# Decoder layer, FFN part: turning the quantised rows of blocks 1 to 7 by transposing DMAs from SBUF to SBUF

## Chip, cores and metric

The kernel runs on one core of one Trainium2 chip, in one launch. The metric is the device time in microseconds (us). Most repeated executions of one kernel lie within 0.3% of each other.

## What is computed

The reference is one post-norm decoder layer over x of 4 x 1024 rows of 512 numbers: attention, a retention-like cross attention, and an FFN whose activations and weights are quantised to 8-bit integers. Each is followed by a residual sum and a layernorm. The change is in the FFN only:

```python
def _act_fake_quant(x, clip_factor):
    scale = sigmoid(clip_factor) * max(abs(x)) / 127.0
    return clip(round(x / scale), -128.0, 127.0) * scale

xq = _act_fake_quant(x, clip_x[0])                       # x: 4096 rows of 512
gate = einsum('bsh,ih->bsi', xq, _weight_fake_quant(w_gate))   # I = 1408
up = einsum('bsh,ih->bsi', xq, _weight_fake_quant(w_up))
h = _act_fake_quant(silu(gate) * up, clip_down[0])
y = einsum('bsi,hi->bsh', h, _weight_fake_quant(w_down))
x = _layernorm(x + y)
```

The scale of h needs the largest |h| over all rows, so every gate and up product comes before the first down product.

## The kernel before

Three phases run one after the other: `attention_phase`, `retention_phase`, `ffn_phase`. The FFN runs from about 1551 us to the end at 1814.5 us of the profiled span. It has a gate/up stage (to about 1716 us) and a down stage.

**Gate/up stage.** The 4096 rows are 8 blocks (`NB`) of 512 rows. A block is four tiles of 128 rows x 512 numbers, each a source `("x", blk, k)`. For each tile:

- SP loads the rows from `x2d` (line 2798) into `lead` or `rows`, in turn by block;
- ACT scales and rounds them to int8 (`f_i`, "round", line 2845);
- DVE or ACT casts them to bf16 integers (`f_xq`, "cast.d" line 2905, "cast.a" line 2850), four buffers;
- TensorE turns the tile by four 128x128 transposes into a PSUM bank (`f_tr`, "turn", line 3015), two banks;
- DVE (block 0, line 2910) or ACT (blocks 1 to 7, line 2855) copies the bank into the block's `f_xqT` ("copy.d", "copy.a"). `f_xqT` has two buffers of 128 x 4 x 512, for even and odd blocks.

With all four tiles of a block in `f_xqT`, TensorE makes 11 pairs (`IT`) of a gate and an up product, each four matmuls with 128x512 operands into one of six PSUM banks (`f_pj`, line 3026). ACT makes the silu of the gate bank (`f_sg`, line 2862), DVE multiplies it by the up bank into `f_h` (line 2923), and DVE takes the largest magnitude of that tile (`f_hm`, line 2928). Five blocks of h stay in SBUF. Blocks 0, 1 and 2 are spilled to `h_scratch` by one DMA of 2816 KB each (line 2809) when their last tile has its maximum.

**Down stage.** After block 7 the maximum over all of h gives the second scale ("top"). Then h is rounded, cast and multiplied by the down weights (lines 3045, 3055), and residual, layernorm statistics and the output follow.

**What sets the order.** `ffn_plan` simulates the FFN with a planned length for each piece of work and writes one list for each engine's queue (SP, ACT, DVE, POOL, PE). Engines then take their list strictly in order. The tile preparation of block b (`turned`) is placed among the gate/up pairs of block b-1, at b-0.6 to b-0.36 for the four turns. The function `lighter()` gives a cast or a copy to ACT when ACT has less planned work waiting than DVE. SP's list holds all DMAs of the phase. `Passed` leaves out a wait that the engine has already passed.

The lines that matter for the turn before (TensorE, and the wait of the first product of a block):

```python
            elif kind == "turn":
                src = key[0]
                w.wait_ge(*made_whole(src))
                if tr.before[src]:
                    w.wait_ge(*copied(tr.before[src]))
                for f in range(4):
                    m = pe.transpose(tbank[tr.at[src]][:, f * P:(f + 1) * P], xqb[xq.at[src]][:, f * P:(f + 1) * P],
                                     identb[:, :])
                m.then_inc(turn_mm, 1)
            elif kind in ("gate", "up"):
                blk, i = key
                for k in range(4):
                    w.wait_ge(*copied(("x", blk, k)))
```

Of the kernel before, what the change touches and what calls it, by code (L numbers as in the profile page):

```python
# [18 lines left out]
IT = I // P  # L19
# [2388 lines left out]
def ffn_plan():  # L2408

    flow = Flow()  # L2410
    flow.rank, flow.alone = FRANK, ("cast.d",)
    put, after = flow.put, flow.after
    pj, tr, xq, i8 = Slots(6), Slots(2), Slots(4), Slots(3)
    done, copier, caster = set(), {}, {}
    T, G, N = [], [], []
    loads = []

    def has(*keys):
        return all(k in done for k in keys)
# [9 lines left out]
    def turned(src, place, ready):  # L2429

        def made():
            xq.give(src)
            copier[src] = "copy.a" if src[1] and lighter() else "copy.d"
            put("ACT" if copier[src] == "copy.a" else "DVE", (copier[src], src), 0.5 if copier[src] == "copy.a" else 0.36, copied,
                lambda: has("sdrmm") if src[1] == 1 else src[1] < 2 or has(("upmm", src[1] - 2, IT - 1)))

        def copied():
            tr.give(src)
            done.add(("copy", src))
        N.append((place - 0.12, lambda: integers(src, 512, ready, lambda: done.add(("whole", src)))))  # L2440
        pe_item(T, place, ("turn", src), 0.24, made, lambda: room(tr) and has(("whole", src)), lambda: tr.take(src))

    def lighter():

        load = {e: max(flow.free[e] - flow.now, 0) + sum(p[1] for p in flow.ready[e]) for e in ("ACT", "DVE")}
        return load["ACT"] + 0.3 < load["DVE"]
# [201 lines left out]
    for e in flow.order:  # L2648
        for it, n in numbered(flow.order[e]).items():
            assert num.setdefault(it, n) == n or it[0] == "top", it  # L2650
    return flow.order, flow.yields, num, copier, caster, pj, tr, xq, i8


def ffn_phase(nc, A, x2d, hd, amax, wsc, wq, keep, out):
    ph = Phase(nc, "f")
    sb = ph.sb
    order, yields, num, copier, caster, pj, tr, xq, i8 = ffn_plan()

    identb, identf, ones, sig = keep.identb, keep.identf, keep.ones, keep.sig
    eps = sb("eps", [P, 1], F32)  # L2660
# [21 lines left out]
    xr_in, out_done = [ph.sem(f"xr_in{i}") for i in range(16)], [ph.sem(f"out{i}") for i in range(16)]  # L2682
    gu_in = [ph.sem(f"gu{i}_in") for i in range(IT)]
    d_in = [ph.sem(f"d{i}_in") for i in range(4)]
    spilled, back_in = ph.sems("spill0 spill1 spill2"), ph.sems("back0 back1 back2")
    turn_mm, gate_mm, up_mm, top_mm, sdr_mm, d_mm = ph.sems("turn_mm gate_mm up_mm top_mm sdr_mm d_mm")
    round_act, cast_act, copy_act, silu_act, sd_act, tn_act = ph.sems(
        "round_act cast_act copy_act silu_act sd_act tn_act")
    top_dve, cast_dve, copy_dve, gsc_pool, h_dve = ph.sems(
        "top_dve cast_dve copy_dve gsc_pool h_dve")  # L2690
    diag_pool, sdr_dve, r_dve, bn_dve, ag_dve, rs_dve = ph.sems("diag_pool sdr_dve r_dve bn_dve ag_dve rs_dve")
# [46 lines left out]
    def place_free(w, src):  # L2738

        if src[0] == "h":  # L2740
            if src[1] >= 2:
                w.wait_ge(d_mm, num[("down", src[1] - 2, 3)])
        elif xq.before[src]:
            w.wait_ge(turn_mm, num[("turn", xq.before[src])])

    def target(src):

        return xqT[src[1] % 2][:, :, src[2] * P:(src[2] + 1) * P]

    def copied(src):  # L2750

        kind = copier[src]
        return (copy_act if kind == "copy.a" else copy_dve), num[(kind, src)]

    def after(key):

# [25 lines left out]
    def sync(sp):  # L2782
        w = Passed(sp)
        for it in order["SP"]:
            kind, key = it[0], it[1:]
            if kind == "rows":
                m, k = key
                i, r0 = place_of(m, k), block_of(m) * 512 + k * P
                if m == 1:
                    for j in range(4):  # L2790
                        w.wait_ge(keep.x2_out[j], 16 * len(HALVES))
                if 2 <= m < NB + 2:
                    w.wait_ge(round_act, num[("round", ("x", m - 2, k))])
                elif m >= NB + 4:
                    w.wait_ge(out_done[i], 16)
                elif m >= NB + 2:
                    w.wait_ge(up_mm, NGATED)
                sp.dma_start(xr[i][:, :], x2d[r0:r0 + P, :]).then_inc(xr_in[i], 16)
            elif kind == "gu":
                i = key[0]  # L2800
                sp.dma_start(wgu[:, i, :, :], wq["gu"][i]).then_inc(gu_in[i], 16)
            elif kind == "d":
                c = key[0]
                sp.dma_start(wd[:, c, :, :], wq["d"][c]).then_inc(d_in[c], 16)
            elif kind == "spill":
                blk = key[0]
                w.wait_ge(h_dve, num[("gated", blk, IT - 1)])
                w.wait_ge(peak_dve, num[("peak", blk, IT - 1)])
                sp.dma_start(hd[blk], hs[place(blk)][:, :, :]).then_inc(spilled[blk], 16)
            elif kind == "back":  # L2810
                m = key[0]
                for lo, _ in ffn_pieces():
                    w.wait_ge(round_act, num[("round", ("h", m, lo))])
                w.wait_ge(spilled[SPILL[m]], 16)
                sp.dma_start(hs[m][:, :, :], hd[SPILL[m]]).then_inc(back_in[m], 16)
            elif kind == "tn":
                m, k = key
                i, r0 = place_of(NB + m, k), SECOND[m] * 512 + k * P
                w.wait_ge(tn_act, num[it])
                sp.dma_start(out[r0:r0 + P, :], xr[i][:, :]).then_inc(out_done[i], 16)  # L2820
        for i in range(16):
            w.wait_ge(out_done[i], 16 * (NB // 4))

    def scalar(act):
        w = Passed(act)
        for it in order["ACT"]:
            kind, key, n = it[0], it[1:], num[it]
            if kind == "init":
                act.activation(scr[:, 0:2], sig[:, :], ACT.Silu)
            elif kind == "round":  # L2830
                src = key[0]
                if i8.before[src]:
                    w.wait_ge(*made_whole(i8.before[src]))
                if src[0] == "x":
                    m, k = src[1:]
                    w.wait_ge(*arrived(m, k))
                    w.wait_ge(top_dve, 4)
                    r = scr[:, 8:9]
                else:
                    m = src[1]  # L2840
                    w.wait_ge(top_dve, 8)
                    if m >= KEEP:
                        w.wait_ge(back_in[m - KEEP], 16)
                    r = scr[:, 9:10]
                act.activation(byte(src), source(src), ACT.Copy, scale=r).then_inc(round_act, 1)  # L2845
            elif kind == "cast.a":
                src = key[0]
                w.wait_ge(round_act, num[("round", src)])
                place_free(w, src)
                act.activation(integer(src), byte(src), ACT.Copy).then_inc(cast_act, 1)  # L2850
            elif kind == "copy.a":
                src = key[0]
                w.wait_ge(turn_mm, num[("turn", src)])
                copy_free(w, src)
                act.activation(target(src), turned_bank(src), ACT.Copy).then_inc(copy_act, 1)
            elif kind == "gated":
                blk, i = key
                w.wait_ge(gate_mm, n)
                w.wait_ge(gsc_pool, 2)
                if n > 3:  # L2860
                    w.wait_ge(h_dve, n - 3)
                act.activation(sg[(n - 1) % 3][:, :], bank[pj.at[("gate", *key)]][:, :], ACT.Silu, scale=gsc[:, i:i + 1]
                               ).then_inc(silu_act, 1)
            elif kind == "norm":
                m, k0 = key
                end = normed_rows(m, k0)[1]
                c, e = 4 * (m % 2) + k0, 4 * (m % 2) + end
                w.wait_ge(init_pool, 1)
                for k in range(k0, end):
                    w.wait_ge(ag_dve, num[("stats", m, k)])  # L2870
                if m >= 2:
                    w.wait_ge(rs_dve, 2 * num[("norm", m - 2, 0)])
                act.activation(sd[:, c:e], ag[m % 2][:, k0:end, 1], ACT.Sqrt, bias=eps[:, 0:1]).then_inc(sd_act, 1)  # L2873
            elif kind == "tn":
                m, k = key
                c, i = 4 * (m % 2) + k, place_of(NB + m, k)
                w.wait_ge(rs_dve, 2 * num[("norm", m, normed_rows(m, k)[0])])
                act.activation(xr[i][:, :], xr[i][:, :], ACT.Identity, bias=mr[:, c:c + 1], scale=rs[:, c:c + 1]  # L2878
                               ).then_inc(tn_act, 1)

    def vector(dve):
        w = Passed(dve)
        for it in order["DVE"]:
# [22 lines left out]
            elif kind == "copy.d":  # L2906
                src = key[0]
                w.wait_ge(turn_mm, num[("turn", src)])
                copy_free(w, src)
                dve.tensor_copy(target(src), turned_bank(src)).then_inc(copy_dve, 1)  # L2910
            elif kind == "gated":
                blk, i = key
# [249 lines left out]
```

## Time and profile before

| | us |
|---|---|
| median of 3 runs | 1816.25 (1816.05 to 1820.79) |
| the profiled execution's own time | 1816.41 |
| its span | 1814.5 |
| TensorE busy in the span | 1673.4 (92%) |
| DVE busy | 1342.6 (74%) |
| ACT busy | 1064.6 (59%) |
| POOL busy | 1067.0 (59%) |
| mean granted TensorE clock | 0.982 of full |

The span runs from the first to the last instruction. The profiled execution took 1.91 us more than its span, and its time lies 0.16 us above the median. Busy shares are averages over three phases with different limits, so the rows below are taken from the FFN alone. Times in them count from the start of the span.

### The profile page before, as it was taken

Reading aid. Unit: us, or ns where it says so; the run is one execution under the profiler, and the core shown is the slowest. Engines: PE = TensorE matmul, PEld = TensorE weight load, DVE = VectorE, ACT = ScalarE, POOL = GpSimd, SP = SyncE. Lnnn points to the kernel's source line nnn. Section 1 sums busy time; section 2 is a strip of 40 time slices with the busy share of each in tenths; the row PEclk is TensorE's granted clock in tenths of the full one; section 3 lists DMA queues with packets and bytes.
Section 4 is the critical chain, followed back from the end, with each engine's and each line's share of the span. In section 5 each row is a group of like instructions: output and inputs, shape, how many; then the busy total and the mean of one; then the engine's idle time right before and its main releaser. Section 6 shows DMA issues by size and latency. Waiting matters only on the chain. (4 is left out here: it accounts for less than half of the span.)

```text
span 1814.5 us, 37213 instructions
## 1 busy us (share of the span) xinstructions
PE 1673.4 (92%) x13410; PEld 761.8 (42%) x13426; DVE 1342.6 (74%) x3006; ACT 1064.6 (59%) x1889; POOL 1067.0 (59%) x1020
## 2 busy tenths in 40 slices
PE   5999999989999999998796999999999998799997
PEld 2433343334433344333233555555555554344443
DVE  6777657786677856677784777778678667788898
ACT  6476555665556655566642557565465454565587
POOL 4088777588685867869862765665675656000044
PEclk9999999999999999999998999999999999899999
DMA  8312102231013310222325223232232131651275
GB/s 289 117 27 82 31 22 57 77 105 30 23 49 90 98 31 24 81 66 59 93 94 167 65 86 103 92 105 96 88 110 77 59 112 48 229 219 49 68 264 207
DMA packets 123039, 172.02 MB, mean 95 GB/s; under 512 B 22376, under 2 KB 73064, under 8 KB 121960
## 3 DMA queue, kind: packets, MB, share of 16 engines
q1 hardware_dynamic: 117192, 160.91, 27.6%
q10 hardware_dynamic: 5664, 8.73, 1.6%
q8 instruction: 107, 1.75, 0.4%
q14 instruction: 76, 0.62, 0.1%
HBM read 106.12 MB, written 38.14 MB: 80 GB/s over the span
## 5 line engine op out<-in xcount | busy, mean ns | idle before, releaser
L1165 DVE CUSTOM_DVE_ANT_0 a_mx<-a_mx,a_mqk 128x128 f32<-128x128 f32 (+3 forms) x512 | 242.2, 512 | 137.0 <-PE a_mx L1365 133.3
L980 ACT ACTIVATE a_P<-a_mx 128x512 f32<-128x512 f32 (+3 forms) x417 | 186.9, 495 | 134.4 <-PE a_mx L1383 75.2
L1379 PE MATMUL a_mx<-a_Qs,a_Ks 128*128 128x512 f16 (+3 forms) x768 | 228.7, 333 | 18.3 <-ACT a_P L980 7.5
L1248 POOL TENSOR_TENSOR a_P<-a_P 128x512 f32<-128x512 f32 (+3 forms) x189 | 183.8, 1000 | 101.4 <-PE a_o L1395 76.7
L1365 PE MATMUL a_mx<-a_Ks,a_Qs 96*128 96x512 f16 (+3 forms) x768 | 223.5, 330 | 5.9 <-DVE a_nm L1165 2.4
L1248 POOL TENSOR_TENSOR a_P<-a_P,share 128x512 f32<-128x512 f32 (+3 forms) x199 | 185.5, 961 | 24.5 <-ACT share L980 18.1
L980 ACT ACTIVATE share<-a_mx 128x512 f32<-128x512 f32 (+3 forms) x303 | 135.9, 495 | 99.5 <-PE a_mx L1383 58.1
L1168 DVE TENSOR_REDUCE a_nm<-a_mx 128x1 f32<-128x512 f32 x256 | 165.0, 683 | 31.9 <-PE a_mx L1365 31.0
L2277 PE MATMUL r_pj<-share,cth 128*128 128x512 f16 x672 | 167.1, 382 | 2.8 <-PEq L123 2.3
L2277 PE MATMUL r_pj<-r_xTh,share 128*128 128x512 f16 x512 | 159.1, 382 | 3.2 <-DVE r_xTl L2123 3.0
L3026 PE MATMUL f_pj<-f_xqT,f_wgu 128*128 128x512 bf16 x688 | 154.5, 379 | 1.6 <-DVE f_xqT L2910 0.8
L1248 POOL TENSOR_TENSOR share<-share,a_P 128x512 f32<-128x512 f32 (+3 forms) x152 | 137.0, 932 | 20.1 <-ACT a_P L980 12.4
L1379 PEld LDWEIGHTS a_mx<-a_Qs,a_Ks 128*128 128x128 f16 x768 | 71.7, 98 | 170.1 <-issue 72.9
L2993 POOL TENSOR_TENSOR lead<-lead,f_sg 128x512 f32<-128x512 f32 x8 | 10.1, 1270 | 183.5 <-DVE f_sg L2943 177.9
L1365 PEld LDWEIGHTS a_mx<-a_Ks,a_Qs 96*128 96x128 f16 x768 | 71.0, 98 | 91.9 <-issue 14.3
L1259 POOL TENSOR_TENSOR a_Ol<-a_on,a_Oh 128x512 f16<-128x512 f32 x32 | 37.9, 1184 | 119.9 <-ACT a_Oh L997 116.3
L1383 PE MATMUL a_mx<-a_mkq,identb 128*128 128x128 bf16 x512 | 107.1, 221 | 0.0
L3026 PEld LDWEIGHTS f_pj<-f_xqT,f_wgu 128*128 128x128 bf16 x704 | 67.6, 98 | 76.9 <-DVE f_xqT L2910 0.7
L1276 PE MATMUL a_mx<-share,a_wkh 128*128 128x512 f16 x256 | 83.8, 391 | 15.9 <-DVE share L1027 15.3
L1276 PE MATMUL a_mx<-share 128*128 128x512 f16 x384 | 97.1, 379 | 1.0 <-DVE a_on L1199 0.9
L2277 PE MATMUL r_pj<-r_xTl,share 128*128 128x512 f16 x256 | 97.6, 381 | 0.0
L2277 PEld LDWEIGHTS r_pj<-share,cth 128*128 128x128 f16 x672 | 62.8, 98 | 75.1 <-issue 5.8
(309 smaller groups left out, 4019.7 us busy)
## 6 DMA issues: line engine op xcount, KB each, us to landing
x_scratch<-rows SPq DMA_DIRECT2D x60, 256.0 KB, 2.1
rows<-x_scratch SPq DMA_DIRECT2D x56, 256.0 KB, 4.3
lead<-in_xT SPq DMA_DIRECT2D x24, 512.0 KB, 4.6
lead<-in_ctxT SPq DMA_DIRECT2D x38, 256.0 KB, 2.8
h_scratch<-f_h SPq DMA_DIRECT2D x3, 2816.0 KB, 9.1
f_h<-h_scratch SPq DMA_DIRECT2D x3, 2816.0 KB, 10.2
a_Ks<-a_kph SPq DMA_DIRECT2D x256, 32.0 KB, 1.9
a_Qs<-a_qph SPq DMA_DIRECT2D x256, 32.0 KB, 1.9
```

The lines of the kernel that those rows point to most:

```text
L980: act.activation(Pf[pf.at[key]][:, off:512], pb[:, off:512], ACT.Exp).then_inc(p_exp, 1)
L1165: dve.tensor_tensor_reduce(bank_of(it)[:, 0:n], bank_of(it)[:, 0:n], mqk[:, 512 - n:512], 1.0, -3e38, ALU.add, ALU.max, nm[:, col:col + 1] ...
L1168: dve.tensor_reduce(nm[:, col:col + 1], bank_of(it)[:, 0:n], AXX, ALU.max).then_inc(max_dve, 1)
L1248: pool.tensor_tensor(total[:, off:512], total[:, off:512], Pf[pf.at[key]][:, off:512], ALU.add).then_inc(add_pool, 1)
L1259: pool.tensor_tensor(Ol[:, g, cs], onb[on.at[key]][:, :], Oh[:, g, cs], ALU.subtract).then_inc(o_lo, 1)
L1276: m = pe.matmul(out, u, v, start=(n == 0), stop=(n == 11))
L1365: pe.matmul(pb[:, 0:n], Qs[s][0:96, j, qt * P:(qt + 1) * P], Ks[s][0:96, j, hf * 512:hf * 512 + n], start=True, stop=True).then_inc(max_mm, 1)
L1379: m = pe.matmul(pb[:, off:512], Ks[s][:, j, kt * P:(kt + 1) * P], Qs[s][:, j, qb * 512 + off:(qb + 1) * 512], start=True, stop=not diag)
L1383: m = pe.matmul(pb[:, off:off + P], identb[:, :], mkq[:, :], start=False, stop=True)
L2277: m = pe.matmul(out, u, v, start=(i == 0), stop=(i == 11))
L2993: pool.tensor_tensor(xr[i][:, :], xr[i][:, :], sg[(NGATED + n - 1) % 3][:, :], ALU.add).then_inc(y_pool, 1)
L3026: m = pe.matmul(bank[pj.at[it]][:, :], wgu[:, i, k0 + k, :], xqT[blk % 2][:, k, :], start=(k == 0), stop=(k == 3))
```

## The change

For the tiles of blocks 1 to 7 the planner no longer plans a "turn" on TensorE and a copy by ACT. When the bf16 tile `f_xq` is whole, it gives SP an item "turnd": a DMA that transposes the 128x512 tile into its place in `f_xqT`, SBUF to SBUF. The planner reckons 1.25 us of SP and 1.8 us more until it has landed. TensorE's products wait for the DMA's semaphore instead of for the copy's. The wait that protects `f_xqT` (`copy_free`) moves from ACT to SP, and the wait for a free `f_xq` buffer is now for the DMA that read it. Block 0 is turned as before.

```diff
         def made():
             xq.give(src)
-            copier[src] = "copy.a" if src[1] and lighter() else "copy.d"
-            put("ACT" if copier[src] == "copy.a" else "DVE", (copier[src], src), 0.5 if copier[src] == "copy.a" else 0.36, copied,
-                lambda: has("sdrmm") if src[1] == 1 else src[1] < 2 or has(("upmm", src[1] - 2, IT - 1)))
+            put("DVE", ("copy.d", src), 0.36, copied)
...
-        N.append((place - 0.12, lambda: integers(src, 512, ready, lambda: done.add(("whole", src)))))
+
+        def landed():
+            xq.give(src)
+            done.add(("copy", src))
+
+        def whole():
+            done.add(("whole", src))
+            if src[1]:
+                put("SP", ("turnd", src), 1.25, lambda: after(1.8, landed),
+                    lambda: has("sdrmm") if src[1] == 1 else has(("upmm", src[1] - 2, IT - 1)))
+        N.append((place - 0.12, lambda: integers(src, 512, ready, whole)))
+        if src[1]:
+            return
         pe_item(T, place, ("turn", src), 0.24, made, lambda: room(tr) and has(("whole", src)), lambda: tr.take(src))
...
+    turn_in = [ph.sem(f"turn{i}_in") for i in range(8)]
...
         elif xq.before[src]:
-            w.wait_ge(turn_mm, num[("turn", xq.before[src])])
+            w.wait_ge(*turned(xq.before[src]))
...
+    def turned(src):
+
+        if src[1]:
+            return turn_in[4 * (src[1] % 2) + src[2]], 16 * ((src[1] + 1) // 2)
+        return turn_mm, num[("turn", src)]
+
     def copied(src):
 
-        kind = copier[src]
-        return (copy_act if kind == "copy.a" else copy_dve), num[(kind, src)]
+        return turned(src) if src[1] else (copy_dve, num[("copy.d", src)])
...
+            elif kind == "turnd":
+                src = key[0]
+                w.wait_ge(*made_whole(src))
+                copy_free(w, src)
+                sp.dma_start_transpose(target(src), xqb[xq.at[src]][:, :]).then_inc(turn_in[4 * (src[1] % 2) + src[2]], 16)
```

**SP's list, start of the FFN.** In these rows `f_wgu` and `f_wd` are the weights of gate/up and of down, `lead` and `rows` the x tiles of even and odd blocks, `f_h` a block of h on its way to `h_scratch`. Before:

```order
771 L2798 DMA rows<-x_scratch 128x512 x4
772 L2804 DMA f_wd<-d_scratch 128x1408 x4
773 L2798 DMA lead<-x_scratch 128x512 x4
774 L2809 DMA h_scratch<-f_h 128x5632
775 L2798 DMA rows<-x_scratch 128x512 x4
```

Now:

```order
771 L2814 DMA rows<-x_scratch 128x512 x4
772 L2820 DMA f_wd<-d_scratch 128x1408
773 L2825 DMA_TRANSPOSE f_xqT<-f_xq 128x4x128
774 L2820 DMA f_wd<-d_scratch 128x1408
775 L2825 DMA_TRANSPOSE f_xqT<-f_xq 128x4x128
776 L2820 DMA f_wd<-d_scratch 128x1408
777 L2825 DMA_TRANSPOSE f_xqT<-f_xq 128x4x128
778 L2820 DMA f_wd<-d_scratch 128x1408
779 L2825 DMA_TRANSPOSE f_xqT<-f_xq 128x4x128
780 L2814 DMA lead<-x_scratch 128x512 x4
781 L2830 DMA h_scratch<-f_h 128x5632
782 L2825 DMA_TRANSPOSE f_xqT<-f_xq 128x4x128 x4
783 L2814 DMA rows<-x_scratch 128x512 x4
```

The four turns of block 1 stand between the loads of the down weights, the x tiles of block 2 come behind them, and the four turns of block 2 stand directly behind the spill of block 0, ahead of the x tiles of block 3. The groups of block 3 and 4 stand in the same way behind the spills of blocks 1 and 2.

**ACT's list, one block.** `f_i` is the int8 tile. Before:

```order
1191 L2845 ACTIVATE f_i<-lead,f_scr 128x512 x2
1192 L2862 ACTIVATE f_sg<-f_pj,f_gsc 128x512
1193 L2855 ACTIVATE f_xqT<-f_tr 128x4x128
1194 L2845 ACTIVATE f_i<-lead,f_scr 128x512
1195 L2862 ACTIVATE f_sg<-f_pj,f_gsc 128x512
1196 L2855 ACTIVATE f_xqT<-f_tr 128x4x128
1197 L2845 ACTIVATE f_i<-lead,f_scr 128x512
1198 L2862 ACTIVATE f_sg<-f_pj,f_gsc 128x512
1199 L2855 ACTIVATE f_xqT<-f_tr 128x4x128
1200 L2862 ACTIVATE f_sg<-f_pj,f_gsc 128x512
1201 L2855 ACTIVATE f_xqT<-f_tr 128x4x128
```

Now:

```order
1187 L2866 ACTIVATE f_i<-lead,f_scr 128x512 x2
1188 L2878 ACTIVATE f_sg<-f_pj,f_gsc 128x512
1189 L2866 ACTIVATE f_i<-lead,f_scr 128x512
1190 L2878 ACTIVATE f_sg<-f_pj,f_gsc 128x512
1191 L2866 ACTIVATE f_i<-lead,f_scr 128x512
1192 L2878 ACTIVATE f_sg<-f_pj,f_gsc 128x512
1193 L2871 ACTIVATE f_xq<-f_i 128x512
1194 L2878 ACTIVATE f_sg<-f_pj,f_gsc 128x512 x8
```

The four copies are gone, and the cast of the fourth tile, DVE's before, is now ACT's. On DVE this is one cast less in each of blocks 1 to 7. On TensorE the 28 turns between the products are gone, and the 704 matmuls of the gate/up stage stand in one row:

```order
+L3048 MATMUL f_pj<-f_xqT,ones 128x128 x4
+L3030 MATMUL f_tr<-identb,f_xq 128x128 x16
+L3041 MATMUL f_pj<-f_xqT,f_wgu 128x512 x704
+L3020 MATMUL f_pj<-identf,f_scr 1x128
```

From the first instruction of the down stage on, the lists of ACT, DVE, PE and POOL are the same as before. SP's differs there in nothing either.

## Rows read from the trace of the kernel before

**Rows 1.** The page, the span in 40 equal slices: TensorE and its clock.

```profile
PE   5999999989999999998796999999999998799997
PEclk9999999999999999999998999999999999899999
```

**Rows 2.** Busy time of each engine, blocks 1, 4 and 7 of gate/up.

```profile
core 0: us, PE busy (x) PEld busy (x) DVE busy (x) ACT busy (x) POOL busy (x), PEclk, DMA share, GB/s
...
1577.80:1597.70 19.90, 19.79 (x103) 9.52 (x104) 16.88 (x26) 11.86 (x20) 0.00 (x0) 1.00 0.52 199
...
1637.50:1657.40 19.90, 19.79 (x104) 9.50 (x105) 16.87 (x26) 11.87 (x20) 0.00 (x0) 1.00 0.20 54
...
1697.20:1716.30 19.10, 19.05 (x88) 8.46 (x87) 15.79 (x22) 7.57 (x11) 0.00 (x0) 1.00 0.01 2
```

**Rows 3.** The chain of waits, block 1 and the start of block 2.

```profile
1577.63 8.15 PE f_pj L3026 x37
1585.78 0.22 PE f_tr L3015 x4
1586.00 1.73 PE f_pj L3026 x8
1587.73 0.22 PE f_tr L3015 x4
...
1591.63 0.22 PE f_tr L3015 x4
...
1597.52 2.54 PE f_pj L3026 x11
```

**Rows 4.** Groups of instructions by shape, 1557 to 1717 us.

```profile
L2923 DVE SCALAR_TENSOR_TENSOR f_h<-f_pj,f_usc,f_sg 128x512 f32<-128x512 f32 x88 | 66.0, 750 | 17.9 <-PE f_pj L3026 12.5 <-ACT f_sg L2862 4.4
L2862 ACT ACTIVATE f_sg<-f_pj,f_gsc 128x512 f32<-128x512 f32 x88 | 60.2, 684 | 53.5 <-PE f_pj L3026 53.5
L2928 DVE TENSOR_REDUCE f_hm<-f_h 128x1 f32<-128x512 f32 x87 | 59.6, 686 | 2.7
L2855 ACT ACTIVATE f_xqT<-f_tr 128x512 bf16<-128x512 bf16 x28 | 16.7, 598 | 14.8 <-PE f_tr L3015 14.8
L2905 DVE CAST f_xq<-f_i 128x512 bf16<-128x512 int8 x28 | 11.8, 420 | 4.8 <-ACT f_i L2845 4.8
```

**Rows 5.** Instructions in order of time: casts of block 1, spill, casts of block 2.

```profile
1564.92 0.43 DVE L2905 CAST f_xq<-f_i 128x512 bf16<-128x512 int8 x1 [0.83 <-ACT f_i L2845]
...
1579.61 0.32 SPq L2809 DMA_DIRECT2D h_scratch<-f_h  x1
1579.97 5.56 SPq L2798 DMA_DIRECT2D rows<-x_scratch  x4
...
1583.89 0.42 DVE L2905 CAST f_xq<-f_i 128x512 bf16<-128x512 int8 x1
...
1589.31 0.42 DVE L2905 CAST f_xq<-f_i 128x512 bf16<-128x512 int8 x1
```

**Rows 6.** DMA issues: KB each, median us from issue to landing.

```profile
h_scratch<-f_h SPq DMA_DIRECT2D x3, 2816.0 KB, 9.1
f_wd<-d_scratch SPq DMA_DIRECT2D x4, 352.0 KB, 8.5
a_Ks<-a_kph SPq DMA_DIRECT2D x256, 32.0 KB, 1.9
```

**Rows 7.** The page, DMA queues: packets, MB, share of 16 engines' span.

```profile
q1 hardware_dynamic: 117192, 160.91, 27.6%
```

**Rows 8.** The x loads of the FFN, from the view of line 2798.

```profile
DMA to landing us min/median/max: 2.6/4.1/10.8
```

**Rows 9.** Instructions in order of time, from the gate/up stage into the down stage.

```profile
1716.36 0.75 DVE L2923 SCALAR_TENSOR_TENSOR f_h<-f_pj,f_usc,f_sg 128x512 f32<-128x512 f32 x1 [0.25 <-PE f_pj L3026]
1717.15 0.69 DVE L2928 TENSOR_REDUCE f_hm<-f_h 128x1 f32<-128x512 f32 x1
...
1719.76 11.74 ACT L2845 ACTIVATE f_i<-f_h,f_scr 128x512 int8<-128x512 f32 x12 [3.58 <-DVE f_scr L2900]
```

**Rows 10.** Busy time of each engine in the down stage.

```profile
1717.00:1757.00 40.00, 33.70 (x140) 14.29 (x141) 33.37 (x61) 31.09 (x34) 12.72 (x10) 0.91 0.82 305
1757.00:1797.00 40.00, 39.26 (x182) 17.25 (x179) 39.31 (x81) 34.84 (x43) 20.28 (x16) 1.00 0.54 188
```

More of the change, by code:

```diff
@@ L2413, in ffn_plan @@
     pj, tr, xq, i8 = Slots(6), Slots(2), Slots(4), Slots(3)
-    done, copier, caster = set(), {}, {}
+    done, caster = set(), {}
     T, G, N = [], [], []
@@ L2650, in ffn_plan @@
             assert num.setdefault(it, n) == n or it[0] == "top", it
-    return flow.order, flow.yields, num, copier, caster, pj, tr, xq, i8
+    return flow.order, flow.yields, num, caster, pj, tr, xq, i8
 def ffn_phase(nc, A, x2d, hd, amax, wsc, wq, keep, out):
@@ L2656, in ffn_phase @@
     sb = ph.sb
-    order, yields, num, copier, caster, pj, tr, xq, i8 = ffn_plan()
+    order, yields, num, caster, pj, tr, xq, i8 = ffn_plan()
     identb, identf, ones, sig = keep.identb, keep.identf, keep.ones, keep.sig
@@ L2684, in ffn_phase @@
     d_in = [ph.sem(f"d{i}_in") for i in range(4)]
+    turn_in = [ph.sem(f"turn{i}_in") for i in range(8)]
     spilled, back_in = ph.sems("spill0 spill1 spill2"), ph.sems("back0 back1 back2")
     turn_mm, gate_mm, up_mm, top_mm, sdr_mm, d_mm = ph.sems("turn_mm gate_mm up_mm top_mm sdr_mm d_mm")
-    round_act, cast_act, copy_act, silu_act, sd_act, tn_act = ph.sems(
-        "round_act cast_act copy_act silu_act sd_act tn_act")
+    round_act, cast_act, silu_act, sd_act, tn_act = ph.sems(
+        "round_act cast_act silu_act sd_act tn_act")
     top_dve, cast_dve, copy_dve, gsc_pool, h_dve = ph.sems(
@@ L2850, in scalar @@
                 act.activation(integer(src), byte(src), ACT.Copy).then_inc(cast_act, 1)
[L2851 to L2855, printed above, removed]
             elif kind == "gated":
@@ L2908, in vector @@
                 w.wait_ge(turn_mm, num[("turn", src)])
-                copy_free(w, src)
                 dve.tensor_copy(target(src), turned_bank(src)).then_inc(copy_dve, 1)
```

## The prediction

> **What bounds the kernel now.** I read the page's slices first. TensorE is busy at 9 tenths in most of them, and its clock shows 8 only in two [rows 1]. Averages over three phases don't tell what one stage is worth, so I went to the table by stretch. In block 1 TensorE is busy 19.79 of 19.90 us at clock 1.00, DVE 16.88, ACT 11.86 [rows 2]. The other blocks that hold turns look the same. Block 7, whose stretch holds 88 matmuls and no turns, takes 19.10 us. The chain of waits then tells whether the turns lie on the path or beside it: it runs along TensorE alone through a block, products, turn, products, and each turn (four transposes) stands in it with 0.22 us [rows 3]. There is no wait for a copy or for x tiles in it. So gate/up is bound by TensorE issuing its list without a gap, and whatever leaves that list shortens the stage, as long as nothing new stops the list.
>
> **What the change removes.** Four turns in each of seven blocks, 28 x 0.22 = **6.2 us** of TensorE's chain. A cross-check: a block with turns takes 19.89 us from product to product (1577.63 to 1597.52) [rows 3], so without its 4 x 0.22 it takes 19.0, and the stretch of block 7 has 19.10 with its drain [rows 2]. ACT loses 28 copies of 598 ns (16.7 us) and the 14.8 us that it sat waiting for turns [rows 4]; it waits for TensorE's products anyway (53.5 us in front of the silus), so this is worth nothing. DVE loses one cast of 420 ns in each of seven blocks, ACT gains it; I cost it at nothing too. ACT then has 7.57 us of silus [rows 2], four roundings and one cast in 19.0 us, far from full.
>
> **Does DVE become the bound?** Its stretch without casts is 15.79 us busy [rows 2]; with three casts 17.05 of 19.0. On average there is room. Three pairs of a block carry a cast: 750 + 686 + 420 ns [rows 4] = 1.86 us against the 1.73 us that TensorE takes for a pair (8 matmuls [rows 3]). DVE falls back by 0.13 us plus the gaps between instructions, under a microsecond in all, and makes it up at some 0.25 us a pair in the others. Six banks hold three pairs, so TensorE has more than one pair of slack. Cover enough; if it failed, the price would be those few tenths a block.
>
> **What the change adds** is 28 transposing DMAs, 28 waits on SP in front of them, and TensorE's wait for them. What counts is when the fourth lands against the start of the block. Call T the time for which one such DMA occupies the queue, and add 1.8 us once from there to the semaphore (the 32 KB copy from SBUF to SBUF lands after 1.9 us, nearly all of it fixed) [rows 6]. No row shows a transposing DMA, so T is bounded. Low end: as plain bytes at the spill's rate, 128 of 2816 KB in 9.1 us = 0.41 us. In the middle: packets of 256 bytes, one per row of a 128x128 part, 512 of them. The main queue's 117192 packets took 27.6% of 16 x 1814.5 us, 68 ns each [rows 7], hence 512 x 68 ns / 16 = 2.2 us. High end: four 128x128 parts one after another, each at the full 1.9 us of the 32 KB copy, 7.6 us. The ends are far apart. I take T about 1.2 us. The nearest row is the SBUF-to-SBUF copy, whose time is nearly all fixed and overlaps with its neighbours; 256-byte packets carry fewer bytes than this queue's mean of 1373, so 68 ns is likely too much for them.
>
> The due times, from a block's start (1577.8):
> - **A plain block (5 to 7).** First cast done at 6.5 (1584.31) [rows 5], then 4T + 1.8 must end by 19.0: T up to 2.7. The last cast ended at 11.9 (1589.73) [rows 5], which leaves 7 us for one turn.
> - **Blocks 2 to 4.** The turns stand behind a spill that is issued 1.8 us into the block and lands 9.1 us later [rows 5, 6], so they begin at 10.9: T up to 1.6. That this queue makes others wait behind the spill is seen in the four loads issued behind it: their issue took 5.56 us [rows 5].
> - **Block 1.** First cast done at 1565.35, 7.4 after the start [rows 5], and three loads of 352 KB of down weights stand between the turns, at the spill's rate 1.14 us each: 7.4 + 3.4 + 4T + 1.8, T up to 1.6.
>
> With T = 1.2 every block is in time by 1.5 us at the tightest place. Queued behind the waits on SP are the x tiles of the next block but one. They go out once the last cast is done, about 12 us into the block, and are wanted 24 us into it; their landing took 4.1 us in the median and 10.8 at most [rows 8]. The down weights move later by about 10 us and are wanted after 1720. TensorE's wait for four semaphores replaces its wait for four copies one for one.
>
> **Down stage.** Its lists are unchanged and start with the last maximum after gate/up [rows 9]. It moves forward as a whole. Its clock dips to 0.91 in the first 40 us [rows 10], where TensorE waits for the maximum and the casts; that pattern moves with it and may shift by some tenths.
>
> **The sum.** -6.2 (turns) + 0 (copies, casts) + 0 (DMAs hidden) = -6.2. From the profiled execution's 1816.41 that gives 1810.2; its time lies 0.16 above the median of the runs, so against the median it is -0.33%.
>
> **A rule of the skill on T.** The Trainium skill, "VectorE: DVE Perf Modes", section "The three transpose paths", gives 1309 ns for a 128x128 bf16 tile by DMA against 390 ns by TensorE. No row here shows the first; four tiles one after another would be T = 5.2 us, an estimate, and by the same sums as in rival B the kernel would take about 1886 us. The Trainium skill, "Advanced Engine Details and Errata", section "X-Bar Transpose (TRN2)", says on the contrary that such DMAs are as fast as regular ones, which would be my low end. TensorE's turn in this trace costs less than the first page has it: 0.22 us for four transposes in the chain [rows 3].
>
> **Rivals.**
> - **A: half hidden.** T between 1.6 and 2.8. At 2.2 (the 256-byte packets) block 1 starts 2.4 us late and the spilled blocks after it as much in turn, not each anew, since a late start also moves the next due time: 5.0 us lost over the four blocks, 1815.2 us. At 2.8 the loss is 11.7, 1821.9. For it: the packet price of rows 7. Against it: that price is a mean over much larger packets.
> - **B: slower.** T above 2.8, the queue becomes the bound of gate/up: a block then takes 8.3 + 4T. At the high end, 7.6, block 1 starts 12.6 + 30.4 - 19.0 = 24.0 late and the other six 19.7 each, +142: 1952 us. It decides from T of about 2.4 on, where losses pass 6.2, and at 3.2 the time is 1831.5. For it: a transpose of 2-byte numbers has to break up rows, and nothing in this trace does so. Against it: the DMA engines are at a share of 0.52 and 0.20 in these blocks [rows 2], so there is room for much more than one packet's work per row.
> - **C: the list does not close up.** TensorE's turns go, but DVE, at 17.05 of 19.0 us, stops it here and there, and half the gain is lost: 1813.
>
> **How the numbers follow.** Within 0.3% (5.4 us, about what a measurement of this kernel can tell from no change) lies close to the forecast, so small losses decide between faster and same. Forecast 0.50, of which 0.04 falls within 0.3% by small losses; A 0.21, same; B 0.25, slower; C 0.04, same. So faster 0.46, same 0.29, slower 0.25. The range starts at 1808.5 (clock and jitter, a little under the forecast) and reaches through A into B, to T about 3.1, at 1828; some 0.2 of B is left out.
>
> **What would show it.** In the profile after: no turn in the chain of gate/up, 704 matmuls from about 1557.9 to 1710.1 us, blocks 19.0 us apart, ACT's silus and DVE's products following at 1.73 us a pair. The transposing DMAs' time from issue to landing should be near 3 us and their packets' sum per DMA near T x 16. Rival A shows as waits of TensorE for a DMA into `f_xqT` at the start of blocks 1 to 4 alone, B as such waits before every block, growing to many us, with a lower clock behind them, C as waits for DVE inside the blocks. I am wrong in the mechanism if gate/up ends before 1710 or after 1712 with no wait for a DMA in it.

## The result, and the profile after

| | before | after |
|---|---|---|
| median (20 runs each) | 1819.88 us (1815.72 to 1825.2) | 1814.23 us (1807.87 to 1819.3) |
| ratio after to before, with its 95% interval | | 0.9974 (0.9964 to 0.9983) |
| profiled execution, span | 1814.5 us | 1817.1 us |
| mean granted TensorE clock | 0.982 | 0.972 |

The changed kernel is faster by 0.26%, 4.7 us with an interval of 3.1 to 6.5; the forecast was 6.1, which this interval still holds. The single executions of either kernel spread by some 10 us (0.5%), far more than the change, so the two spans can't be compared: the FFN began at 1551.4 us in the one and at 1556.8 in the other, before anything that was changed. Stages can be compared. The median of the three runs that the forecast was set against, 1816.25, lies 3.6 us under that of twenty, which is why 1810.2 sits below the measured time by more than the ratio says. One execution behind the ratios further down, of e14, took 2167.89 us at a mean granted clock of 0.746 and is in none of them.

The chain of waits of the changed kernel, first profile, gate/up stage and the end of it:

```profile
1563.01 0.44 DVE f_xqT L2925
1563.44 0.09 issue
1563.54 154.01 PE f_pj L3041 x704
...
1717.57 0.76 DVE f_h L2938
```

Where TensorE's products and turns took turns before [rows 3], one piece of 704 matmuls stands, with no wait for a DMA in it. That is the list that the prediction said would show. But 154.01 us is not the 152.2 that it asked for (1557.9 to 1710.1). By its own sign of a wrong mechanism (gate/up ends after 1712 with no wait for a DMA in it) this profile even speaks against it: the stage ends at 1717.54, which is 1712.2 when the 5.4 us of the later start are taken off. The table by stretch shows the difference (same columns as [rows 2]):

```profile
1563.50:1567.40 3.90, 3.87 (x10) 1.38 (x11) 0.79 (x2) 0.69 (x1) 0.00 (x0) 0.50 1.05 391
1567.40:1582.60 15.20, 15.20 (x72) 6.89 (x71) 13.36 (x21) 8.92 (x14) 0.00 (x0) 1.00 0.78 202
1582.60:1601.60 19.00, 19.00 (x90) 8.62 (x88) 16.52 (x26) 10.41 (x17) 0.00 (x0) 1.00 0.81 245
1639.70:1658.70 19.00, 19.00 (x90) 8.63 (x89) 16.53 (x25) 10.41 (x16) 0.00 (x0) 1.00 0.33 88
```

The first 3.9 us ran at a granted clock of 0.50 (1.2 GHz): 10 matmuls where 18 fit at 1.00 (2.4 GHz). From there on a block takes 19.0 us and TensorE is busy in all of it. DVE has 16.5 of 19.0 us, ACT 10.4. The DMA share in a block with a spill rose from 0.52 to 0.81, in one without from 0.20 to 0.33.

The transposing DMA, in the view of its line and in the page's list of queues (compare [rows 7]; the page's count of packets, with those under 512 bytes, is the first row of the second block):

```profile
L2825 SPq DMA_TRANSPOSE f_xqT<-f_xq x28: 1188/1262/2184, 1571.9 to 1690.3; - x28
...
DMA to landing us min/median/max: 2.4/2.5/5.9
```

```profile
DMA packets 138270, 175.67 MB, mean 97 GB/s; under 512 B 37608, under 2 KB 88296, under 8 KB 137192
...
q1 hardware_dynamic: 132424, 164.58, 28.8%
```

It keeps SP for 1.26 us and lands 2.5 us after issue. The queue has 15232 more packets, 544 for each of the 28: the 512 of 256 bytes that I had reckoned with, and 32 small ones. The queue's packets took 28.8% of 16 x 1817.1 us against 27.6% of 16 x 1814.5, 360 us more: 12.9 us per DMA over 16 engines, **T = 0.80 us**. This is an estimate from shares that differ between profiles of one kernel: the same sum over the second profiles (29.1% of 16 x 1810.6 us in e1, 27.5% of 16 x 1818.7 us in e2, both below) gives 0.95.

The down stage did not merely move. From the last gate/up matmul to the end it took 98.1 us before and 99.6 now, and its first 36 matmuls:

```profile
1722.21 10.70 PE L3060 MATMUL f_pj<-f_wd,f_hq 128*128 128x512 bf16 x36 [1.72 <-DVE f_hq L2921]
```

took 10.70 us. In the profile of before they took 9.28 us. So the profiled pair has -6.2 (turns) + 1.9 (slow start of gate/up) + 1.4 (down stage).

### The profile page after: what moved, and what is told of

Same layout as the page of the kernel before. It is cut to its first block and busy times, and to the rows that moved or that the text cites. A ratio compares the mean times of both kernels' runs of the same rounds, so it can differ in the third digit from the quotient of the medians.

```text
span 1817.1 us, 36999 instructions
## 1 busy us (share of the span) xinstructions
PE 1679.7 (92%) x13314; PEld 759.2 (42%) x13314; DVE 1339.3 (74%) x2999; ACT 1052.8 (58%) x1868; POOL 1066.3 (59%) x1020
## 3 DMA queue, kind: packets, MB, share of 16 engines
q1 hardware_dynamic: 132424, 164.58, 28.8%
## 5 line engine op out<-in xcount | busy, mean ns | idle before, releaser
L2878 ACT ACTIVATE f_sg<-f_pj,f_gsc 128x512 f32<-128x512 f32 x88 | 60.4, 686 | 75.5 <-PE f_pj L3041 75.5
```

## Experiments

Theory P: the turns' 6.2 us are gained whole, the DMAs are hidden, and what is missing is TensorE's clock at both ends of gate/up. Theory Q: the DMAs cost something themselves. All ratios are to the kernel before, run beside it. The gate/up stage is counted from its first matmul to the end of its last one, the down stage from there to the end of the span. The traces of before, e12, e13 and e14 lack the record of the first gate matmul (the first one recorded comes 0.32 us behind the copy before it, in the others 0.10), so their gate/up reads 0.2 us too short.

### Second profiles, no turn at all, and the turn twice

**e1** is the changed kernel again, **e2** the kernel before again.

> The changed kernel once more, for a second profile of it. Theory P (the turns are off the path for good, what is missing of the 6.2 us is TensorE's clock): the 704 gate/up matmuls take 152.1 us plus only what the first stretch at half clock costs, and the time against the kernel before is -3 to -6.5 us. Where the clock comes back early, as it did in the profile of before, the stage takes 152 us and the down stage 98.2. Theory Q (the transposing DMAs cost something systematically, by slowing TensorE's or DVE's reads or by late landings): the stage is again 154 us with a TensorE wait or stretched matmuls inside the blocks, at full clock.

Measured: 0.9970 (0.9959 to 0.9982). Block 1 and block 7 in its table by stretch:

```profile
1578.00:1597.00 19.00, 19.00 (x90) 8.62 (x88) 16.52 (x25) 10.40 (x16) 0.00 (x0) 1.00 0.79 236
...
1691.90:1711.00 19.10, 19.08 (x89) 8.45 (x87) 15.81 (x22) 7.56 (x11) 0.00 (x0) 1.00 0.05 20
```

Gate/up took 152.1 us, no stretch at half clock in it. This is as P said for the stage. But the down stage took 99.6 us, not the expected 98.2, and there my expectation missed.

> The kernel before once more, for a second profile and as a measure of the spread. Theory P: 1.000 to its own runs within 0.1%; gate/up takes 158.3 us if its first matmuls run at full clock and up to 160.2 if they run at half clock until 10 us into the FFN, as in the profile of after; the down stage between 98.2 and 99.6. Theory Q: gate/up 158.3 and the down stage 98.2 again, since only the change brings the slow stretches.

Measured: 1.0002 (0.9990 to 1.0014), gate/up 158.4 us, down stage 98.4.

**e3** leaves the transposing DMAs out (blocks 1 to 7 multiply what lies in the buffers). The products wait for the casts in place of the DMAs, and POOL fills the second buffer with ones once, at the start of the FFN.

```diff
-                sp.dma_start_transpose(target(src), xqb[xq.at[src]][:, :]).then_inc(turn_in[4 * (src[1] % 2) + src[2]], 16)
...
-            return turn_in[4 * (src[1] % 2) + src[2]], 16 * ((src[1] + 1) // 2)
+            return made_whole(src)
```

> The changed kernel with the 28 transposing DMAs left out (blocks 1 to 7 multiply whatever lies in the two buffers). Theory P (DMAs hidden completely): same time as the changed kernel within 1 us. Theory Q (they cost): faster than the changed kernel by about 1.5 us, that is -6.2 us against the kernel before in place of -4.7.

Measured: 0.9980 (0.9968 to 0.9991), gate/up 152.1 us, down stage 99.1. The interval overlaps that of the changed kernel, and not a tenth of a microsecond is between e3 and e1 in gate/up. The DMAs cost nothing on the path; Q falls. Its median lies 1.6 us above that of e1, more than the 1 us that P allowed. About 1.1 us of it is e3's own: POOL's fill ran from 1558.90 to 1560.86 us, and the DVE cast inside it took 1.49 us in place of 0.42, so that gate/up began 7.6 us into the FFN and not 6.5.

**e4** is the kernel before with each turn of blocks 1 to 7 made twice.

```diff
-                for f in range(4):
+                for f in list(range(4)) * (2 if src[1] else 1):
```

> The kernel before with each turn of blocks 1 to 7 made twice on TensorE (56 turns in place of 28). The price of a turn on the path is 0.22 us by the chain: +6.2 us, 158.3 to 164.5 us for gate/up, +0.34%. If TensorE's chain were only apparent and DVE or ACT held the pace, less than half of that; if a turn costs less than the chain says (0.17 us, as -4.7 us over 28 would have it), +4.7 us.

Measured: 1.0039 (1.0027 to 1.0051), +7.1 us (4.9 to 9.3). Its chain shows the price of the second set of four:

```profile
1615.06 0.45 PE f_tr L3015 x8
1615.50 1.73 PE f_pj L3026 x8
1617.23 0.45 PE f_tr L3015 x8
```

0.45 us for eight against 0.22 for four. Gate/up took 166.2 us, 1.5 of it for a start at half clock as in the first profile of after; the rest is 6.3 over the kernel before (158.4 in e2). The term of 6.2 us holds in both directions.

### How much room the DMAs have

**e5** and **e6** put one and three more transposing DMAs of the same size in front of each, into scratch. The cut is from e6; e5 has `range(1)`.

```diff
+                for _ in range(3):
+                    j = sum(extras)
...
+                    sp.dma_start_transpose(hq[1][:, j % 11, :].rearrange("p (f t) -> p f t", f=4), xqb[xq.at[src]][:, :]
+                                           ).then_inc(spare_in[j % 11], 16)
```

> The changed kernel with each transposing DMA preceded by one more of the same size into a scratch tile, so 8 in place of 4 a block. Each took SP 1.26 us to issue in the profile of after. Theory P (what bounds the turns is SP's issue, there is room for it): eight issues take 10 us, from 6.5 us into the block to 17.8 with landing, of 19.0: hidden, within 2 us of the changed kernel (blocks behind a spill may be a little late). Theory R (the DMA engines are the limit, at a T well above 1.3): blocks start late by 8T - 10.7 and the time rises by more than 10 us.

Measured: 0.9994 (0.9978 to 1.0010), some 4 us slower than the changed kernel, so not hidden, and not 10 us either. Its timeline of TensorE shows where:

```profile
1561.48 19.15 PE L3052 MATMUL f_pj<-f_xqT,f_wgu 128*128 128x512 bf16 x88 [0.56 <-DVE f_xqT L2936]
1582.63 39.83 PE L3052 MATMUL f_pj<-f_xqT,f_wgu 128*128 128x512 bf16 x176 [2.00 <-DMA f_xqT<-f_xq]
1624.18 19.15 PE L3052 MATMUL f_pj<-f_xqT,f_wgu 128*128 128x512 bf16 x88 [1.72 <-DMA f_xqT<-f_xq]
1643.70 76.23 PE L3052 MATMUL f_pj<-f_xqT,f_wgu 128*128 128x512 bf16 x352 [0.36 <-DMA f_xqT<-f_xq]
```

Gate/up took 158.4 us, 6.3 more than in e1: 4.1 us of waits, the rest longer products, most of it a stretch at half clock behind the first wait. The waits stand in front of blocks 1, 3 and 4 only, where down weights or a spill share SP's list and the queue: this is the picture of rival A, drawn out by doubling the DMAs. The trace of the changed kernel (first profile) shows how much room there was. The fourth tile landed 2.7 us ahead of the first product of block 1, 4.4, 3.1 and 5.1 us ahead for blocks 2, 3 and 4, and 5.5 to 5.6 for blocks 5 to 7. Four more issues of 1.3 us take 5.2 us, which fits in front of the last three alone.

> The same with three extra ones, 16 a block. Theory P: SP needs 16 x 1.26 = 20.2 us a block, more than the block's 19.0, and begins 6.5 us into it: blocks of about 6.5 + 20.2 + 1.3 = 28 us, 7 x 9 = +63 us against the changed kernel. Theory R: the queue's T decides, 8.3 + 16 T: with the 0.8 us a DMA that the queue's share gives in the profile of after that would be 21 us a block and +15 us, with 2.2 us 43 us a block and +170.

Measured: 1.0427 (1.0397 to 1.0457), 83 us over the changed kernel; gate/up 237.7 us, 31.2 a block. The chain, with two extra issues (L2833), then the last of the block's sixteen DMAs from issue to landing, and the next block's beginning:

```profile
1616.26 1.27 SPq L2833
1617.52 0.04 issue
1617.57 1.27 SPq L2833
1618.83 0.04 issue
1618.88 2.49 DMA f_xqT<-f_xq
1621.37 0.25 issue
1621.61 1.44 PE f_pj L3052 x3
```

SP issues one each 1.31 us, 21.0 us for sixteen, and the DMA engines keep up: they land after 2.5 us in the median, and from 1616 to 1621 us the engines are busy at a share of 0.53. So SP's issue is the limit and not T, as P said. The size was off (+63 expected). After each wait TensorE ran its first matmuls at half clock (in block 1 24 of them took 7.65 us), which puts the casts later, and by those SP: the first cast behind a wait ended 7.8 to 8.8 us into the block where 6.5 was expected. The pace of 1.31 in place of 1.26 adds 0.8 us a block. From the queue's share (30.7% of 16 x 1895.8 us, 1299 us more than before, over 112 DMAs) T comes to 0.73 us.

### The clock at the two ends of gate/up

**e7** adds 40 matmuls behind the last product of the retention phase, where TensorE sits idle for 10 us. **e8** adds 17 between gate/up and the down stage besides.

```diff
+        w.wait_ge(z_dve, len(UNITS) * 2)
+        for _ in range(40):
+            pe.matmul(ret[0][:, :], zh[:, 0, 0:P], zh[:, 1, :], start=True, stop=True)
...
+                pe.matmul(turns[1][:, :].bitcast(F32), xqT[1][:, 0, 0:P], xqT[1][:, 1, :], start=True, stop=True)
```

> The changed kernel with 40 matmuls of 128x512 behind the last product of the retention phase, into a free PSUM bank, where TensorE otherwise sits idle for 10 us before the FFN. Theory P (clock): the granted clock stays at 1.00 to within 2 us of the FFN's start or falls only shortly, the 6.5 to 6.7 us from the FFN's start to the first gate matmul shrink by up to 1 us, and no gate matmul runs at half clock, where in one of two profiles of the changed kernel 2 us went that way: -0.5 to -2 us in the mean. Theory N (no such link): same time within 0.5 us, and the first 10 us of the FFN at 0.50 as before.

Measured: 0.9974 (0.9961 to 0.9988), level with the changed kernel. The clock was up when the FFN began but fell 1.3 us into it, where TensorE waits between small steps, and rose at 4.75; from the FFN's start to the first gate matmul it took 6.1 us against 6.7 (after) and 6.5 (e1). A few tenths in the profile, nothing in the times.

> The kernel e7 with 17 more such matmuls in the gaps of TensorE between gate/up and the down stage. Theory P (the down stage of the kernels without turns took 99.2 to 99.6 us against 98.2 to 98.4 because their stretch at half clock, 3.5 to 10.2 us after the last gate/up matmul, is 6.8 us long): the stretch goes or shortens, the 36 first down matmuls take 8 us in place of 10.7, and the down stage takes 98.2 us or less: -1.3 us against e7. Theory S (the down stage is bound by DVE's casts, the clock only decorates it): 99.5 us as before.

Measured: 0.9966 (0.9951 to 0.9980). The down stage took 97.3 us in place of 99.6, 2.3 less, more than P asked for. The first down matmul began 4.68 us behind the last gate/up matmul, in e7 as here, so the fillers held nothing up. Theory S falls: the down stage's start is bound by TensorE's clock. Gate/up had a slow start here (153.2), and in the times e8 can't be told from e7.

**e9** adds 8 small matmuls in the gaps between the FFN's start and the first gate matmul.

```diff
+                pe.matmul(bank[5][:, 0:P], identf[:, :], ones[:, :], start=True, stop=True)
...
+                idle((1, 2, 1, 2)[src[2]])
```

> The kernel e8 with 8 small matmuls (128x128, f32, into a bank that nobody reads) in the gaps of TensorE between the FFN's start and the first gate matmul. In the profile of e8 the clock fell 1.75 us after the FFN's start and the first four to five us of gate/up ran at half. Theory P: with the gaps filled it stays up; from the FFN's start to the first gate matmul takes 5.9 to 6.3 us, the 704 matmuls 152.1, the down stage 97.3: 1 us less than e8 where e8 met the slow start, -0.40 to -0.45% against the kernel before. Theory N: filling these gaps delays the turns that wait behind the fillers as much as the clock gives back, same as e8.

Measured: 0.9954 (0.9936 to 0.9972). In its profile gate/up took 152.1 us and the down stage 97.3; the way to the first gate matmul was not shorter, 6.6 us, with 3.4 us of it at half clock, so this part missed. In e12 and e13, which have the same fillers, the clock stayed at 1.00 there and the way took 6.0 us.

**e10** and **e11** are the kernel before, profiles three and four.

> The kernel before, a third profile. Six kernels without turns took 99.2 to 99.7 us for the down stage with one stretch at half clock of 6.8 us, three with turns took 98.2 to 98.4 with 3.3 us there. Theory L (luck: where the clock falls against the last gate/up matmul differs from execution to execution, 2.5 to 3.75 us in the six, 4.0 to 4.75 in the three, and decides between the two): this kernel shows the long stretch and 99.5 in some executions too. Theory Y (the change brings it): 98.2 to 98.4 again.

> The kernel before, a fourth profile: as for the third. If both show 98.2 to 98.4, luck alone has 1 chance in 462 of sorting eleven profiles so, and the change is to blame for 1.2 us.

Measured (one execution each, 1816.76 and 1821.68 us): both have gate/up 158.4 us, and the down stage took 98.1 us. Now the clock of the down stage's first microseconds, from the table by stretch. Before (first profile), from the last gate/up matmul at 1716.3:

```profile
1716.30:1720.30 4.00, 0.67 (x4) 0.37 (x3) 2.66 (x7) 0.54 (x1) 0.00 (x0) 1.00 0.73 221
1720.30:1723.80 3.50, 2.80 (x7) 1.00 (x8) 1.98 (x4) 3.50 (x5) 0.00 (x0) 0.51 0.94 330
1723.80:1727.30 3.50, 3.50 (x17) 1.57 (x16) 2.27 (x4) 3.50 (x5) 0.00 (x0) 1.00 0.45 107
```

The changed kernel (e1), from 1711.0:

```profile
1711.00:1714.50 3.50, 0.65 (x3) 0.37 (x3) 2.46 (x7) 0.08 (x1) 0.00 (x0) 0.98 0.75 221
1714.50:1721.20 6.70, 5.54 (x14) 1.87 (x15) 4.24 (x8) 6.70 (x8) 0.00 (x0) 0.50 0.56 199
1721.20:1724.50 3.30, 3.30 (x17) 1.53 (x16) 1.60 (x3) 3.30 (x4) 0.00 (x0) 1.00 0.94 328
```

And e9, from 1714.8, where TensorE was kept busy:

```profile
1714.80:1718.30 3.50, 3.50 (x17) 1.51 (x16) 2.47 (x7) 0.10 (x1) 0.00 (x0) 1.00 0.64 183
1718.30:1725.00 6.70, 6.11 (x28) 2.48 (x27) 4.24 (x8) 6.70 (x8) 0.00 (x0) 1.00 0.61 219
```

TensorE is nearly idle for the 4.7 us of the maximum and the first casts. The clock falls to half during this pause, at 4.0 us in the one and at 3.4 in the other. In the first it is back 7.4 us after the last matmul, in the second only at 10.2, after 14 matmuls in 6.7 us. All profiles, us from the last gate/up matmul:

| kernels | clock fell | back | down stage |
|---|---|---|---|
| with turns: before, e2, e4, e10, e11 | 3.9 to 4.6 | 7.3 to 8.0 | 98.1 to 98.4 |
| without: after, e1, e3, e5, e6, e7, e14 | 2.4 to 3.6 | 9.2 to 10.4 | 99.1 to 99.7 |
| filled: e8, e9, e12, e13 | not in the first 19 | | 97.3 |

### With the clock filled in both

**e12** is the kernel before with all the fillers of e9, **e13** e9 again, **e14** the changed kernel again.

> The kernel before with all the fillers of e9 (40 matmuls behind the retention phase, the small ones at the FFN's start, 17 between gate/up and the down stage); the turns stay on TensorE. With the clock's stretches filled in both, what is left between this kernel and e9 is the change alone. Theory P (the change is worth its full 28 turns, and a shorter gate/up moved the clock's fall to a place that cost 1.2 us of it back): gate/up 158.4, down stage 97.3, and e9 is faster than this one by 6.2 us, 0.34%. Theory S (something else in the change costs too): the gap to e9 is 5 us or less.

> The kernel e9 once more, on the same chip as e12: gate/up 152.1, down stage 97.3, 0.9954 times the kernel before within its interval, 6.2 us under e12 (theory P) or 5 and less (theory S).

> The changed kernel once more, beside them: gate/up 152.1 (or up to 154.1 where the clock comes back late), down stage 99.5 with the half clock 2.5 to 3.75 us behind the last gate/up matmul and 6.8 us long; 0.997 times the kernel before; 2.2 us over e13 plus what the start costs.

Measured: e12 0.9989 (0.9978 to 1.0001), e13 0.9950 (0.9933 to 0.9967), e14 0.9963 (0.9950 to 0.9977). In the profiles gate/up takes 158.2 us in e12 and 151.9 in e13, the down stage 97.3 in both: 6.3 us apart in the stage that was changed and level in the other. The medians, 1817.7 and 1810.9, differ by 6.8 us, and the ratio of the two ratios is 0.9961. The times alone, of 12 and 6 executions that spread by some 6 us, would hardly rule out the 5 us of theory S (here: something else in the change costs too); the profiles do. So theory P: with the clock out of the way the change is worth its 28 turns. e14 took 99.6 us for its down stage. e9 and e13 lie 0.46% and 0.50% under the kernel before. Their intervals overlap those of the changed kernel without fillers.

## Where the prediction was right, and the step that failed

- **The bound and the gain.** TensorE's chain of products and turns bounded gate/up; 28 turns at 0.22 us were worth 6.2 us of the stage. Right: 158.1 to 158.4 us became 151.9 to 152.1 wherever no stretch of it ran at half clock and no DMA was added. The lower ends are the traces without the first record, so it is 158.4 against 152.1 throughout, and e12 against e13 shows the same in the times.
- **T.** I took 1.2 us between 0.41 and 7.6. The queue's shares give 0.7 to 1.0, about twice what the plain bytes would take at the spill's rate. The 256-byte packets were as reckoned, but 68 ns a packet was far too much: 12.9 us over 544 gives 24. What limits a row of such DMAs is SP's issue, one per 1.31 us, which I had left out as a resource; by luck it is near the value I took for T. The 1.8 us of landing beyond T holds (2.5 in all). The tightest place was block 1 with 2.7 us of room, not blocks 2 to 4 with 1.5. Rivals A and B fell for the kernel as it is. e5 shows A's waits at twice the DMAs, and e6 shows waits before every block at four times, with SP's issue as the limit and not the queue.
- **Rival A's price.** It was too low by the prediction's own due times. They count from each block's start, so at T = 2.2 a spilled block lasts 10.9 + 8.8 + 1.8 = 21.5 us and loses 2.5 each time: 2.4 + 3 x 2.5 = 9.9 us and 1820.1, not 5.0 and 1815.2. In e5, where it is SP's issue that counts, blocks 1 to 4 began 21.2, 20.7, 20.9 and 19.5 us behind the block before, so the losses did come anew.
- **The rule of the skill.** The Trainium skill, "VectorE: DVE Perf Modes", "The three transpose paths", has 1309 ns for a 128x128 tile by DMA. I had taken that four times in a row, 5.2 us and 1886 us for the kernel, and this step was wrong: DMAs of four such tiles each followed each other at 1.31 us. No run here transposes a single 128x128 tile by DMA. The Trainium skill, "DMA: Bandwidth & Descriptors", section "Issuing engines are not separate DMA queues", says that the sequencer's time to initiate a DMA is usually small relative to the DMA itself. Here it is not: 1.26 us of SP, of the 2.5 from issue to landing, against a T of 0.7 to 1.0.
- **Rival C.** DVE at 16.5 of 19.0 us never stopped TensorE.
- **The step that failed** is "It moves forward as a whole", said of the down stage, with "that pattern moves with it and may shift by some tenths" of its clock: a term that the sum had at nothing. The clock did fall only some tenths earlier against the last product, but with that the stretch at half clock became twice as long, 6.8 us in place of 3.4, and lay over the first down matmuls. The down stage took 99.1 to 99.7 us in the seven profiles without turns, 98.1 to 98.4 in the five with them, 1.3 us more in the mean. With the pause filled it took 97.3 in both kernels, so the clock is the whole of this difference. That is a fifth of the gain given back: -6.2 + 1.3 = -4.9. The times fit it, -4.7 on record and -5.5 and -6.7 in e1 and e14, but their intervals reach from 3.1 to 9.1 and hold 6.2 as well, so it is the profiles that show the loss. The forecast lay so close to the bound of 0.3% that this fifth decided between faster and same. The direction was right, the sum one term short.

Why the clock falls earlier without turns is shown only in part. In the profiles without a slow start of gate/up the clock rose 0.9 to 2.5 us ahead of the first gate product. From there to its fall behind gate/up it was 163.8 us in before, e2, e10 and e11, and 157.0 in e1, e3, e7 and e14: the full-clock stretch got 6.8 us shorter where the stage got 6.2 shorter, and so the fall came 0.6 us nearer to the last product. e5 has no turns but a gate/up as long as before, and there it was 163.8 us from rise to fall again (with the short stretch at half clock behind its first wait in between). It fell at 3.6 us, against 3.9 in e10, because the clock had risen 1.8 us ahead of the first product in the one and 1.6 in the other, and it has the long stretch. These rows speak for the stage's length, and not the missing turns as such, as what moves the fall; no run changed the length alone. The edge lies between these two profiles, from 3.6 to 3.9 us, where the half-clock stretch changes from 6.8 to 3.4, and e10 is at most 0.3 us on its good side. A stage shortened by another amount could come out on either side. What fixes the two lengths from rise to fall no run here shows. Twelve profiles sorted five to seven with no exception, which luck alone does once in 792 times. The kind of run in which gate/up starts at half clock (after, e4, e8) appeared on both sides; it is luck of the execution and costs 1 to 2 us.

## What to carry to other kernels

A turn (four transposes) that stands in TensorE's chain costs its 0.22 us each time. It goes to a DMA at no price on the path, if the DMAs' due times leave room: count the issuing engine's 1.3 us per DMA, not only bytes, and look at what large transfers stand in front. When a stage is shortened, look at the pause behind it: TensorE's clock falls there, and where it falls can give back a part of the gain, here a fifth. Filling such a pause with matmuls into an unused bank held nothing up, since the engine only waits. It was worth 2.3 us of the down stage in the profiles (99.6 to 97.3) of the changed kernel and 0.9 of the kernel before.

## What the runs showed of the hardware beyond that

A transposing DMA of a 128x512 bf16 tile from SBUF to SBUF kept SP for 1.26 us in the median, where a plain load of 256 KB keeps it for 0.43 (in single cases up to 1.6). Issued back to back (e6) they follow each other at 1.31 us and land after 2.5 us; behind a spill of 2816 KB one took 5.9 us (after). A DVE cast took 1.49 us in place of 0.42 while POOL filled a tile (e3). Gate/up and down matmuls of the same size ran at 0.216 us apart at clock 1.00 and at half that pace at 0.50, and the level changed at places that differ from execution to execution: against the last gate/up matmul, by 0.7 us over five profiles with turns and by 1.2 over seven without.
